# Attention in an AdaLN block: the causal mask of heads 4, 5 and 6 moved from TensorE's scores to GpSimd on the exponentials

## What is computed

```
q, k = rope(rmsnorm(x wq)), rope(rmsnorm(x wk))
s = (q * mult) (k * mult)^T
s = s - 1e30 * (column later than row)        # the causal mask
p = softmax(s)
o = (p v) wo
```

## Time and profile before

| | |
|---|---|
| three runs | 1123.93, 1124.40, 1126.92 us; median 1124.4 |
| the profiled execution | 1132.29 us, of which 1130.5 are its span |
| granted TensorE clock, mean over the span | 0.965 |
| TensorE, matmuls | 1018.9 us busy, 90% |
| ScalarE | 963.0 us, 85% |
| VectorE | 896.2 us, 79% |
| GpSimd | 785.7 us, 70% |

### The profile page before, as it was taken

One profiled execution on the slowest core, in us unless ns is written; L12 is line 12 of the kernel. 1 busy time (PEld: TensorE's weight loads), 2 busy tenths in 40 slices (PEclk: granted clock), 3 DMA queues, 4 the chain that ended last, 5 costly groups with the idle time before them and its releaser, 6 DMA issues. The chain is left out here.

```text
span 1130.5 us, 27394 instructions
## 1 busy us (share of the span) xinstructions
PE 1018.9 (90%) x7294; PEld 780.5 (69%) x7294; DVE 896.2 (79%) x2757; ACT 963.0 (85%) x3517; POOL 785.7 (70%) x1197
## 2 busy tenths in 40 slices
PE   5899999999999999999999999999898779989700
PEld 3588888888888888888888888888554434558600
DVE  5788888889998889888888888886768746767647
ACT  6999999999999999999999999997797748888424
POOL 6655578877787877777777777777356675656654
PEclk9999999999999999999999999999999988999955
DMA  5410000100000100000000000000442322320158
GB/s 151 132 34 13 14 17 26 37 25 23 24 23 27 35 15 13 16 16 15 16 16 16 14 16 15 16 15 18 126 112 92 97 77 65 90 68 26 37 188 271
DMA packets 53849, 57.91 MB, mean 51 GB/s; under 512 B 8108, under 2 KB 42783, under 8 KB 53700
## 3 DMA queue, kind: packets, MB, share of 16 engines
q1 hardware_dynamic: 36612, 35.11, 10.5%
q0 software_dynamic: 8640, 16.87, 4.5%
q10 hardware_dynamic: 8448, 4.20, 1.3%
HBM read 33.08 MB, written 23.97 MB: 50 GB/s over the span
## 5 line engine op out<-in xcount | busy, mean ns | idle before, releaser
L753 ACT ACTIVATE squares<-unit 128x128 f32<-128x128 f32 x1024 | 273.3, 303 | 3.6 <-PE unit L1225 3.4
L565 POOL TENSOR_TENSOR roped<-roped,rope_b 128x512 f32<-128x512 f32 x132 | 175.1, 1327 | 91.7 <-DVE rope_b L1085 89.3
L753 ACT ACTIVATION_READ_ACCUMULATOR squares<-unit 128x1 f32 x1024 | 235.2, 236 | 0.0
L1567 POOL DMA_INDIRECT y_rows<-y_out,place_y x142 | 152.2, 1072 | 94.7 <-DVE y_out L1989 49.4
L1085 DVE TENSOR_TENSOR rope_b<-unit,sin_sb 128x512 f32<-128x512 f32 x256 | 174.4, 681 | 14.6 <-ACT squares L753 12.3
L731 ACT ACTIVATE probs<-scores,rr 128x256 f32<-128x256 f32 x256 | 124.3, 485 | 43.5 <-issue 27.4
L1046 DVE SCALAR_TENSOR_TENSOR acc<-pv,den,acc 128x128 f32<-128x128 f32 x448 | 146.2, 341 | 0.3
L1312 PEld LDWEIGHTS unit<-ident_wr,roped 128*128 128x128 f32 x1024 | 117.9, 141 | 31.6 <-ACT k_t L770 13.0
L1312 PE MATMUL unit<-ident_wr,roped 128*128 128x128 f32 x1024 | 135.2, 275 | 1.6 <-POOL roped L565 1.5
L1975 DVE TENSOR_TENSOR hid_lo<-hidden,hid_hi 128x512 f16<-128x512 f32 (+1 forms) x144 | 92.3, 685 | 54.1 <-ACT hid_hi L1675 34.5
L574 POOL TENSOR_TENSOR roped<-roped,rr 128x1024 f32<-128x1024 f32 x64 | 121.5, 1899 | 13.0 <-DVE roped L1120 12.2
(11 more groups left out here) (304 smaller groups left out, 3061.3 us busy)
## 6 DMA issues: line engine op xcount, KB each, us to landing
shared<-y_rows SPq DMA_DIRECT2D x16, 512.0 KB, 5.6
x_all<-in_L_attn_x SPq DMA_DIRECT2D x32, 128.0 KB, 2.2
h_late<-in_L_ffn_W SPq DMA_DIRECT2D x16, 256.0 KB
out_x<-hidden ACTq DMA_DIRECT2D x16, 256.0 KB, 3.4
rope_b<-x_rows SPq DMA_DIRECT2D x13, 258.0 KB
tile_x<-x_rows SPq DMA_DIRECT2D x12, 258.0 KB
y_rows<-y_out,place_y POOLq DMA_INDIRECT x142
ga_b<-mod_dram SPq DMA_DIRECT2D x32, 64.0 KB
```

The source lines that it names most:

```text
L565: pool.tensor_tensor(out=roped[parity][:, u, heads], in0=roped[parity][:, u, heads], in1=rope_b[:, u % 2, heads], op=ALU.add)\
L753: nc.scalar.activation(squares[:, c * D:(c + 1) * D], UN[0][:, c * D:(c + 1) * D], ACT.Square, accum_out=ssq[parity][:, u * H + c:u * H + ...
L1567: pool.indirect_dma_start(out=y_rows, out_offset=bass.IndirectOffsetOnAxis(ap=place_y[i % (2 * SLOTS)][:, s:s + 1], axis=0), in_=y_out[at] ...
```

## The change

For heads 4, 5 and 6 (`ZEROED`) TensorE leaves out the mask product, and makes the two blocks of the first 128 keys with one product of 256 columns in place of two of 128. In `probs` the two diagonal blocks of such a head then hold unmasked exponentials. GpSimd sets the masked half of both to zero with one `affine_select` of 128 by 256, which waits for the head's exponentials and raises the new semaphore `masked`. TensorE's product of values and exponentials of these heads waits for `masked` as well. The three selects are put into GpSimd's stream directly in front of `add(4)`, `add(5)` and `add(6)`. They run wherever C is live, in iterations 2 to 33.

```diff
--- before.py
+++ after.py
@@ -247,7 +247,7 @@
             ct_ready mod_done mod_copied guard_done mod_stored wvt_done wvt_ready wvo_done hi_done
             split_done wvo_scaled wvo_hi_done tx_done p_done tr_done vw_done s_done o_done ht32_done
             hhi_done h_ready sq_done ropea_done rope_done add_done q_added qs_done tr_copied vals_ready exp_done
-            den_done acc_done x2_done stat_done mv_done chain_done guess_done newton_step rr_done off_done xn_ready router_in
+            den_done acc_done x2_done stat_done mv_done chain_done guess_done newton_step rr_done off_done masked xn_ready router_in
             iota_done scattered0 scattered1 filled mv2_done stat2_done xn2_done
             rows_copied h2t_done h2t_copied rt_done route_step route_exp px_done count_done
             scored gapped gap_exp w_den_done first_weight chose counted_a counted second_weight rows_tagged place_e_done place_k_done
@@ -305,6 +305,7 @@
         BACK_AT = {H_AT: 1, H_AT + 1: 0}
         ROUTED = {1: 0, 2: 1}
         HH = H // 2
+        ZEROED = (4, 5, 6)
 
         PIECE_FROM, HI_AT, LO_AT = 2, 5, 7
 
@@ -594,6 +595,13 @@
                     pool.indirect_dma_start(
                         out=x_rows, out_offset=bass.IndirectOffsetOnAxis(ap=at, axis=0),
                         in_=rows[k][:, j, t, :], in_offset=None).then_inc(S[f"scattered{k}"], 16)
+
+                def zero_ahead(h):
+
+                    wait(pool, "exp_done", 2 * (H * (n - 2) + h + 1))
+                    blocks = probs[:, h % NPR, :].rearrange("p (a c) -> p a c", c=P)[:, 0:TT + 1:TT, :]
+                    pool.affine_select(out=blocks, in_=blocks, compare_op=ALU.is_ge, fill=0.0, base=0,
+                                       pattern=[[0, TT], [1, P]], channel_multiplier=-1).then_inc(S["masked"], 1)
 
                 now = ST and not (isinstance(n, int) and n - 6 == LAST - 1)
                 rest = not isinstance(n, int) or 0 <= n - 7 < LAST - 1
@@ -640,6 +648,8 @@
                     pool.tensor_tensor(out=score[:, :, :], in0=e_lg[:, :, :],
                                        in1=e_rec[:, :].rearrange("p (t o) -> p t o", o=1).to_broadcast([P, TT, E]),
                                        op=ALU.mult).then_inc(S["scored"], 1)
+                if C:
+                    zero_ahead(4)
                 if A:
                     add(4)
                 if now:
@@ -651,6 +661,8 @@
                     pool.tensor_tensor(out=w[:, :, 1:2], in0=w[:, :, 0:1],
                                        in1=e_gap[:, :].rearrange("p (t o) -> p t o", o=1), op=ALU.mult)\
                         .then_inc(S["second_weight"], 1)
+                if C:
+                    zero_ahead(5)
                 if A:
                     add(5)
                 if RT:
@@ -659,6 +671,8 @@
                     wait(pool, "gap_exp", b)
                     pool.tensor_tensor(out=gap[:, :].rearrange("p (t o) -> p t o", o=1), in0=top_s[:, :, 1:2],
                                        in1=top_s[:, :, 0:1], op=ALU.subtract).then_inc(S["gapped"], 1)
+                if C:
+                    zero_ahead(6)
                 if A:
                     add(6)
                 if RT:
@@ -1235,6 +1249,8 @@
                     if h == 0:
                         wait(pe, "vals_ready", TT * (b + 1))
                     wait(pe, "exp_done", 2 * (g + 1))
+                    if h in ZEROED:
+                        wait(pe, "masked", len(ZEROED) * b + ZEROED.index(h) + 1)
                     wait(pe, "acc_done", TT * (g - 1))
                     o, pr, v = OP[h % 2], probs[:, h % NPR, :], vals[parity]
                     if RT and h + 1 in ROUTED:
@@ -1264,11 +1280,16 @@
 
                         diagonal = s[:, 0:2 * T].rearrange("p (a c) -> p a c", a=TT)[:, :, 0:P]
                         mask = causal_bf[:, :].rearrange("p (o c) -> p o c", o=1).to_broadcast([P, TT, P])
-                        nc.tensor.matmul(s[:, P:T], k[:, h, 0:P], q[:, h, P:T], start=True, stop=True)
-                        nc.tensor.matmul(diagonal, ident_bf[:, :], mask, start=True, stop=False)
-                        nc.tensor.matmul(s[:, 0:P], k[:, h, 0:P], q[:, h, 0:P], start=False, stop=False)
-                        nc.tensor.matmul(s[:, T:T + P], k[:, h, P:T], q[:, h, P:T], start=False, stop=True)\
-                            .then_inc(S["s_done"], 1)
+                        if h in ZEROED:
+                            nc.tensor.matmul(s[:, 0:T], k[:, h, 0:P], q[:, h, 0:T], start=True, stop=True)
+                            nc.tensor.matmul(s[:, T:T + P], k[:, h, P:T], q[:, h, P:T], start=True, stop=True)\
+                                .then_inc(S["s_done"], 1)
+                        else:
+                            nc.tensor.matmul(s[:, P:T], k[:, h, 0:P], q[:, h, P:T], start=True, stop=True)
+                            nc.tensor.matmul(diagonal, ident_bf[:, :], mask, start=True, stop=False)
+                            nc.tensor.matmul(s[:, 0:P], k[:, h, 0:P], q[:, h, 0:P], start=False, stop=False)
+                            nc.tensor.matmul(s[:, T:T + P], k[:, h, P:T], q[:, h, P:T], start=False, stop=True)\
+                                .then_inc(S["s_done"], 1)
                     if A:
 
                         w, u = 2 * NU * n + h, h // 2
```

## The result

The changed kernel takes 1162.9 us in the median of 4 runs (1161.0 to 1164.9), the kernel before 1125.7 in the median of its 4: a ratio of 1.033, 95% interval 1.030 to 1.036, or 37.3 us more. The forecast was 1164, that is 40 us more, with a range of 1150 to 1176.

The account below looks back on a forecast made before the run. TensorE was taken as the bound, made to wait for GpSimd's second select: 37.1 us for iterations 6 to 31, 1.6 for 2 to 5, 1.3 for 32 and 33, together 40.0 on 1124.4, giving 1164 us, range 1150 to 1176.

Parts of the forecast that it names:

- the wait at head 4: TensorE's product for head 4: new wait of 0.88 us for the first select, product 0.64 us later than before.
- the saving swallowed: TensorE's 0.12 us a head, at most 11.5 us overall, lies in front of head 5's wait and is lost there.
- the step on head 6: Third select ends about 526.85, product due about 527.3: no wait; VectorE's additions and last product move by at most 1.44.
- The ends: Attention's first and last iterations: 0.36 each in 2 to 4, 0.56 in 5; 1.14 in 31; 32 and 33 together +1.3 us.
- The signs: Iterations 25.5 to 25.7 us apart, TensorE waits about 0.9 us at heads 4 and 5, none at 6, selects about 0.45 us.
- The step that failed: TensorE sets the pace: work taken from its stream shortens the iteration, any wait put in lengthens it one for one.
- rival 3: All selects come in time, TensorE keeps the 11.5 us saving: 1113 us; chance 0.07.
- Rival 1: GpSimd's selects stretched to 0.80 us by VectorE through shared SBUF interfaces: 1174 us; chance 0.12.
- Rival 2: Only head 4 late, if the indirect DMA does not hold GpSimd: 0.52 us an iteration, 1141 us; chance 0.10.

Follow-up runs that it names:

- kept product: Changed kernel with TensorE keeping the mask product and four score products for all heads, selects and waits unchanged: ratio to the kernel before 1.032, iteration 25.38 us.
- moved select: Changed kernel with head 5's select moved from behind the scatter and second weight to directly behind add(4): ratio to the kernel before 1.018, iteration 24.82 us.
- single heads: Changed kernel with only head 4, 5 or 6 in ZEROED, its select at its place: ratios to the kernel before 1.011, 1.031 and 1.012.
- saving alone: Changed kernel without selects and their waits, heads 4, 5 and 6 left unmasked: ratio to the kernel before 0.998, iteration 24.13 us.
- head 4 alone: Changed kernel with only head 4 handed to GpSimd, its select at its place: ratio to the kernel before 1.011, iteration 24.58 us.

## Why the prediction was right, and where its steps were off

- **The mechanism** was the one forecast: the second select, behind `add(4)`, the scatter and the second weight, sets the iteration; the wait at head 4 is hidden behind it, no wait at head 6, the saving swallowed. The kept product, the moved select and the single heads show each part by itself.
- **The size** was 1.44 us an iteration forecast, 1.22 measured. The term that was mis-sized is the time from the second weight to TensorE: the select took 0.41, not 0.47; it started 0.15 after the start of the second weight, not 0.20; TensorE followed 0.10 after its end, not 0.12. That is 0.13. The other 0.08 come from a wait that the step on head 6 had in view and did not count: the last product stood 0.74 behind head 6's (0.67 and 0.07 of waiting for VectorE) and the next scores 0.74 behind it; now both distances are 0.67. Of these two 0.07, one is used up again by the late start behind head 5's own wait. In the 24 iterations of the table above that makes 29.2 in place of 34.6.
- **The ends**: iterations 2 to 5 were forecast at 1.6 and gave 1.4; iterations 31 to 33 with the rest of 30 were forecast at 3.9 (1.44 + 1.14 + 1.3) and gave 3.3. Together 40.0 forecast, 34.1 by the traces, 37.3 by the medians. The difference between the last two lies within the interval (33.7 to 40.4 us) and within what the experts' stretch varies. So that 1164 came within 1.1 us of 1162.9 is in part luck: the attention, on which the whole forecast was built, grew by 6 us less than forecast.
- **The signs** were met in kind and not all in size. Iterations were to be 25.5 to 25.7 us apart and are 25.37. The waits were to be about 0.9 us each; by the starts of the rows they are 0.69 and 0.84, in the brackets 0.53 and 0.67, and the profile names no releaser; that it is the select is shown by its ends, 0.10 before, and by the run with the second select moved. The selects took 0.41, not 0.45. ScalarE's idle time went from 1.44 to 2.60 us an iteration.
- **The step that failed** is the first one: "what is taken out of its stream comes off the iteration". The saving alone gave 2 us of 10.6. A second loop over VectorE was as long. It did no harm to the forecast, since the saving was swallowed anyway. It would have spoilt rival 3, which gave 1113 us for selects in time: the run that does this took 1.003, not 0.99.
- **Rival 1** named a contention that is there and doesn't meet the selects: they were not stretched (398 to 457 ns). It works in both directions. GpSimd's `add(5)` holds VectorE's `one_hot`, and VectorE holds GpSimd's additions: the 2182 ns that the rival set out from, and 16 additions of 1.65 us in place of 1.27, each start just behind an instruction of VectorE with two operands in SBUF. In the kernel before:

```profile
30.59 1.22 DVE L878 TENSOR_TENSOR wvo_lo<-k_t,wvo_hi 128x1024 f16<-128x1024 f32 x1
...
30.75 2.18 POOL L565 TENSOR_TENSOR roped<-roped,rope_b 128x512 f32<-128x512 f32 x1 [1.04 <-DVE rope_b L1085]
```

```profile
166.93 0.68 DVE L1128 SCALAR_TENSOR_TENSOR w_lo<-h_late,w_hi 128x512 f16<-128x512 f32 x1
...
167.09 1.65 POOL L565 TENSOR_TENSOR roped<-roped,rope_b 128x512 f32<-128x512 f32 x1 [0.16 <-DVE rope_b L1085]
```

Both additions end 1.12 to 1.13 us after the end of VectorE's instruction. The Trainium skill's rule that the two contend when VectorE's instruction has two SBUF inputs ("GPSIMD Engine Reference", Key points) agrees with those rows, and with `one_hot`: 0.17 us alone, 0.69 beside `add(5)`.
- **Rival 2**, only head 4 late, was said to give 0.52 an iteration; head 4 alone gives 0.43 (a kernel that lacks the other two heads' saving, so not quite rival 2's). With the second select early the third one came into play instead, which rival 2 had left out: 0.67.

## What to carry to other kernels

Work handed to an engine with idle time is free only at a place where that engine is idle early enough: write down, for each handed-over tile, when the producer's own order lets it finish and when the consumer asks, and move it by whole places in the order. Waits in a row didn't add up here, since GpSimd's order in front of the late select did not hang on TensorE's earlier waits; the latest decided, and a fix of one showed the next. A bound engine at 100% busy may still be one of two loops of nearly equal length; a product of 0.46 us that started 0.07 late, where its like take 0.39, was the only sign on TensorE, and taking work off the bound engine alone is the test.

## What the runs showed of the hardware that I had not expected

- An instruction of VectorE with two SBUF operands was held until the GpSimd addition beside it had ended: 32 columns took 0.17 us alone, 0.69 with `add(5)` ending 0.04 before it, and 0.78 when `add(5)` was 0.09 later. The other way round, an addition of GpSimd that started within such an instruction of VectorE took 1.65 or 2.18 us in place of 1.27. In these traces whichever started first held the other. `acc` and `rope_b`, with one operand in PSUM, kept their 0.34 and 0.68.
- `affine_select` in place on 128 by 256 f32 took 0.41 us, against 0.29 for 128 by 128.
- A product that had to wait ran 0.46 in place of 0.39 us, and the next product started 0.30 after it, not 0.22; a wait on TensorE cost some 0.07 beyond itself here.
